# A macaron block on one core: query and key halves laid out through DRAM, with a ring of three loaded batches

## What is computed

```python
x = L0_attn_x                                    # (16, 256, 128)
x = x + 0.5 * ffn_block(layernorm(x))            # phase 0
x = x + linear_attention(layernorm(x))           # phase 1
x = x + 0.5 * ffn_block(layernorm(x))            # phase 2
# ffn_block: h = ln1(x); x += softmax_attention(h), 16 heads of 8, causal;
#            h = ln2(x); x += mixture(h), 8 experts, the best 2 per token, hidden 256
# linear_attention: q, k = elu(.) + 1; sums of k v and of k over the tokens so far,
#            out = (q . sum(k v)) / (q . sum(k)), then Wo
```

## Time and profile before

| | us |
|---|---|
| median of 3 runs | 1413.6 (1412.59 to 1418.59) |
| the profiled execution, its own time | 1418.66 |
| its span, first to last instruction | 1416.9 |
| mean granted TensorE clock, share of full speed | 0.912 |
| busiest engines | DVE 1115.8, PE 1085.8, ACT 839.7, POOL 548.4 |

### The profile page before, as it was taken

How to read it: one execution, slowest core, us unless ns; L and a number is a source line. 1 busy time by engine, 2 the same in 40 slices (tenths; PEclk the granted TensorE clock), 3 DMA queues, 4 the chain that set the end, 5 groups by cost and what they waited for, 6 DMA issues and landing times.

```text
span 1416.9 us, 37025 instructions
## 1 busy us (share of the span) xinstructions
PE 1085.8 (77%) x12412; PEld 819.6 (58%) x12412; DVE 1115.8 (79%) x2411; ACT 839.7 (59%) x1311; POOL 548.4 (39%) x681
## 2 busy tenths in 40 slices
PE   4688888888854998476877868989888888549980
PEld 3566666666643666255655546857666666436660
DVE  6868889999965887677577767779999999658875
ACT  2457777777843555244656544668777787535550
POOL 6620255555563666201000004002555555636661
PEclk9899999999966999688999987999999999769995
DMA  8911111111102332201033310011111111023326
GB/s 292 412 48 38 43 46 49 51 43 51 53 20 61 86 90 69 82 30 34 7 77 79 79 43 19 0 28 45 50 49 45 51 53 47 26 57 88 87 72 187
DMA packets 124880, 98.71 MB, mean 70 GB/s; under 512 B 41584, under 2 KB 116848, under 8 KB 124784
## 3 DMA queue, kind: packets, MB, share of 16 engines
q1 hardware_dynamic: 103216, 72.68, 17.7%
q0 software_dynamic: 9088, 18.76, 4.0%
...
## 4 chain that ended last, share of the span: by engine, by line
DVE 29%; PE 24%; issue 20%; ACT 9%; POOL 6%; DMA 6%; SPq 3%; DVEq 1%; ACTq 1%; POOLq 0%
DVE negm L1058 6%; PE banks L311 4%; POOL ys L1464 4%; SPq L1552 3%; PE banks L293 3%; DVE p_lo L1277 2%; DMA kst<-k_all 2%; DVE negm L1062 2%; ACT pf L866 2%; DVE pf L1284 2%; DVE x_all L1017 2%; PE banks L434 2%; ACT p_hi L732 2%; PE banks L430 2%; PE banks L466 2%
## 5 line engine op out<-in xcount | busy, mean ns | idle before, releaser
L715 ACT ACTIVATE pf<-banks 128x1536 f32<-128x1536 f32 x128 | 185.7, 1451 | 121.0 <-PE banks L455 119.9
L1070 DVE TENSOR_TENSOR p_lo<-pf,p_hi 128x1536 f16<-128x1536 f32 x128 | 223.9, 1749 | 3.2 <-ACT p_hi L732 3.0
L1464 POOL DMA_INDIRECT ys<-q_all,dest x156 | 151.4, 970 | 115.8 <-ACT q_all L872 90.9
L732 ACT CAST p_hi<-pf 128x1536 f16<-128x1536 f32 x128 | 188.7, 1474 | 2.0
L1415 POOL DMA_INDIRECT xs<-n_all,slot x128 | 164.7, 1287 | 54.9 <-issue 37.6
L1058 DVE TENSOR_REDUCE negm<-banks 128x4 f16<-128x1024 f32 x128 | 156.0, 1219 | 28.7 <-PE banks L434 20.3
L1441 POOL TENSOR_SCALAR rs<-mv 128x2 f32<-128x2 f32 x32 | 44.3, 1385 | 346.0 <-DVE mv L1113 295.3
L455 PEld LDWEIGHTS banks<-ident,negm 128*128 128x128 f16 x1536 | 119.7, 99 | 78.1 <-issue 4.4
L455 PE MATMUL banks<-ident,negm 128*128 128x128 f16 x1536 | 150.1, 221 | 0.0
L448 PE MATMUL banks<-qst,kst 128*128 128x512 f16 x384 | 148.1, 386 | 2.1 <-ACT pf L715 2.1
L434 PE MATMUL banks<-kst,qst 128*128 128x128 f16 x1536 | 129.7, 221 | 0.0
...
## 6 DMA issues: line engine op xcount, KB each, us to landing
...
```

The costliest lines, as they stand in the source:

```text
L715: nc.scalar.activation(pf[:, g % 2, :, :, :].rearrange(flat), banks_t[:, :, :].rearrange("p a b -> p (a b)"), ACT.Exp, scale=HD ** -0.5).t ...
L732: nc.scalar.copy(p_hi[:, g % 2, :, :, :].rearrange(flat), pf[:, g % 2, :, :, :].rearrange(flat))\
L1070: nc.vector.tensor_tensor(lo, pf[:, g % 2, :, :, :].rearrange(flat), hi, ALU.subtract)\
L1464: nc.gpsimd.indirect_dma_start(ys, bass.IndirectOffsetOnAxis(ap=dest[:, t % YB, h:h + 1], axis=0), y_out[:, t % YB, h, :], None).then_inc( ...
```

## The change

- `sel`, the spreading matmuls and their four copies are gone; so are `q_all` and `k_all`. A DRAM tensor `qk_d` takes their place, in head order and with three blocks of 8 rows a head instead of four (96 partitions in use of 128, KR).
- In the front, ACT issues 2 stores a batch (one high block of the queries, one of the keys) right after `qk_high`, SP 4 (the other blocks) after `qk_low`: 6 DMAs of 64 KB. The halves have three places (RB).
- The core's tiles have three places, and a load is of a whole batch: 4 + 1 + 1 DMAs, all issued by SP, after `turned` and `values` of the batch three before. SP issues the loads only after the last store of the front. ACT issues none in phase 1's core.
- The front's buffers and banks are doubled; PE turns two batches ahead. DVE's order changes at the start: it waits for the second part of rstd ahead of step 0, computes the third part's statistics in step 1, and waits for it in step 4. In phase 1 `pair_in` stands in even steps. All loops over the front are written out.
- In phase 0 the clears come first on DVE (`qst` with three places, and a tile `zeros` of its own for xs); SP loads w3 and clears xs behind the loads of batches 0 to 2. The wait for the zeros ahead of phase 0 is gone (the scatter's own stays).
- SP issues the last 8 loads of ys of phase 1 between the stores. PE's loop over the core is written over three batches.

```diff
-LOADS = 16 * 5
+RB = 3
+KR = 3 * GH * HD
+STORES = 16 * 6
+LOADS = 16 * 6
...
-        ht = sb("ht", [P, T * P])
-        q_all = sb("q_all", [P, B, G, T * P], F16)
-        k_all = sb("k_all", [P, B, G, T * P], F16)
+        xn = sb("xn", [P, 2, T, P])
+        ht = sb("ht", [P, 2, T * P])
         v_all = sb("v_all", [P, B, T, H, VC], F16)
-        kst = sb("kst", [P, G, T * P], F16)
-        qst = sb("qst", [P, G, GH, T * P], F16)
-        v_hl = sb("v_hl", [P, T, H, VC], F16)
+        kst = sb("kst", [P, RB, G, T * P], F16)
+        qst = sb("qst", [P, RB, G, GH, T * P], F16)
+        v_hl = sb("v_hl", [P, RB, T, H, VC], F16)
+        zeros = sb("zeros", [P, ZR * RW])
+        x_nats = sb("x_nats", [P, XB, 2, RW])
...
-        qk_hi, qk_lo = [a[:, :, :, :, :].rearrange("p a b c d -> p (a b c d)")[:, 0:2 * 2 * T * P]
-                        .rearrange("p (n k m) -> p n k m", n=2, k=2) for a in (p_hi, p_lo)]
+        qk_hi, qk_lo = [a[:, :, :, :, :].rearrange("p a b c d -> p (a b c d)")[:, 0:RB * 2 * T * P]
+                        .rearrange("p (n k m) -> p n k m", n=RB, k=2) for a in (p_hi, p_lo)]
...
+        qk_d = nc.dram_tensor("qk_d", [B, 2, G * GH, 3, HD, T * P], F16).ap()
...
             def front_qk(ph, b):
-                if not (isinstance(b, int) and b == 0):
-                    pe.wait_ge(ph["qk_out" if ph["soft"] else "full_in"], b)
+                if b >= 2:
+                    pe.wait_ge(ph["qk_out" if ph["soft"] else "full_in"], b - 1)
                 for k in range(2):
-                    ins = nc.tensor.matmul(psum[2][:, k * 256:(k + 1) * 256], w_qk[ph["w"]][:, k, :], ht[:, :],
-                                           start=(k == 0), stop=True, skip_group_check=True)
+                    ins = nc.tensor.matmul(psum[2 + 3 * (b % 2)][:, k * 256:(k + 1) * 256], w_qk[ph["w"]][:, k, :],
+                                           ht[:, b % 2, :], start=(k == 0), stop=True, skip_group_check=True)
                 ins.then_inc(ph["qk_done"], 1)
-            def front_spread(ph, b, buf):
-                pe.wait_ge(ph["qk_out"], b + 1)
-                for k in range(2):
-                    for g in range(G):
-                        n = 2 * k + g // 2
-                        if g % 2 == 0 and n in (0, 3) and not (isinstance(b, int) and b == 0):
-                            if n == 0:
-                                pe.wait_ge(ph["act_spread"], ph["n"] * (3 * B) + b * 3)
-                            else:
-                                pe.wait_ge(ph["dve_spread"], ph["n"] * B + b)
-                        bank = (psum[3:] + [bank_pv])[n]
-                        for part, src in enumerate((qk_hi, qk_lo)):
-                            ins = nc.tensor.matmul(bank[:, g % 2 * 256:(g % 2 + 1) * 256],
-                                                   sel[:, k, part, g, :, :, :].rearrange("p a b c -> p (a b c)"),
-                                                   src[:, buf, k, :], start=(g % 2 == 0 and part == 0),
-                                                   stop=(part == 1), skip_group_check=True)
-                        if g % 2:
-                            ins.then_inc(ph["spread_done"], 1)
...
+            def front_step(ph, b):
                 front_v(ph, b)
                 front_qk(ph, b)
-                if not (ph["soft"] or first or second):
-                    front_carry(ph, b - 2, buf)
-                if not last:
-                    front_turn(ph, b + 1)
-                if not first:
-                    if not ph["soft"]:
-                        front_keys(ph, b - 1, 1 - buf)
-                    front_spread(ph, b - 1, 1 - buf)
-                    if not ph["soft"]:
-                        front_state(ph, b - 1, 1 - buf)
+                if not ph["soft"] and b >= 2:
+                    front_carry(ph, b - 2, b % 2)
+                if b + 2 < B:
+                    front_turn(ph, b + 2)
+                if not ph["soft"] and b >= 1:
+                    front_keys(ph, b - 1, (b - 1) % 2)
+                    front_state(ph, b - 1, (b - 1) % 2)
             def front(ph):
...
+            def batch_in(ph, place):
+                ring, n = place
+                pe.wait_ge(ph["loaded"][ring], LOADS * (used(ph, ring, n) + 1))
+            def natural(ph, b, g, place):
                 mask = maskb[:, :, :].rearrange("p a b -> p (a b)")
                 later = not (isinstance(b, int) and b == 0 and g == 0)
-                pe.wait_ge(ph["qk_loaded"][g // 2], ph["n"] * (LOADS * B) + LOADS * (b + 1))
+                if g == 0:
+                    batch_in(ph, place)
...
+                for b in range(4):
+                    iteration(ph, b, at_batch(b), place=b)
+                with pe.Fori(0, (B - 7) // RB) as i:
+                    for n in range(RB):
+                        iteration(ph, i * RB + (4 + n), at_loop(i, n))
+                for b in range(B - 3, B):
+                    iteration(ph, b, at_batch(b), last=(b == B - 1))
+                at = at_batch(B - 1)
...
-            def spread_out(ph, b, which=range(3)):
-                for n in which:
-                    dst, part = (q_all, k_all)[n // 2], n % 2
-                    sc.wait_ge(ph["spread_done"], ph["n"] * (4 * B) + 4 * b + n + 1)
-                    nc.scalar.copy(dst[:, b, 2 * part:2 * part + 2, :].rearrange("p a b -> p (a b)"),
-                                   psum[3 + n][:, :]).then_inc(ph["act_spread"], 1)
...
+                if b >= RB:
+                    sc.wait_ge(ph["stored"][ring], STORES * used(ph, ring, b // RB))
...
+            def store_high(ph, b):
+                sc.wait_ge(ph["hi_in"], ph["n"] * B + b + 1)
+                for k in range(2):
+                    nc.scalar.dma_start(qk_d[b, k, :, 0, :, :], qk_hi[:, b % RB, k, :])\
+                        .then_inc(ph["stored"][b % RB], 16)
...
+            def front_step(ph, b):
+                v_high(ph, b)
...
+                qk_high(ph, b)
+                store_high(ph, b)
...
+                for ring in range(RB):
+                    sc.wait_ge(ph["stored"][ring], STORES * used(ph, ring, len(range(ring, B, RB))))
...
-            def next_k(ph, b, hf):
-                gs = slice(2 * hf, 2 * hf + 2)
-                nc.scalar.dma_start(kst[:, gs, :], k_all[:, b + 1, gs, :]).then_inc(ph["qk_loaded"][hf], 16)
...
+            def front_step(ph, b):
                 if not ph["soft"] and b >= 2:
                     state_own(ph, b - 2)
                 v_low(ph, b)
-                if not last:
-                    front_ht(ph, b + 1)
-                if not (last or before_last):
-                    front_norm(ph, b + 2)
-                qk_elu(ph, b, buf)
-                qk_low(ph, b, buf)
-                if not first:
-                    spread_out(ph, b - 1)
+                if b + 2 < B:
+                    front_ht(ph, b + 2)
+                if b + 3 < B:
+                    front_norm(ph, b + 3)
+                qk_elu(ph, b)
+                qk_low(ph, b)
...
             def front(ph):
                 if ph is phases[0]:
+                    flat = "p n a b c -> p (n a b c)"
+                    nc.vector.memset(qst[:, :, :, :, :].rearrange(flat).bitcast(F32), 0.0)
+                    nc.vector.memset(v_all[:, :, :, :, HD:HD + 1].rearrange("p a b c d -> p (a b c) d"), 1.0)
+                    nc.vector.memset(zeros[:, :], 0.0).then_inc(cleared, 1)
                     ve.wait_ge(x_in[0], 16)
                 front_stats(ph, 0)
-                if ph is phases[0]:
-                    nc.vector.memset(v_all[:, :, :, :, HD:HD + 1].rearrange("p a b c d -> p (a b c) d"), 1.0)
-                    nc.vector.memset(qst[:, :, :, :].rearrange("p a b c -> p (a b c)"), 0.0).then_inc(cleared, 1)
                 ve.wait_ge(ph["rstd"], 1)
                 front_norm(ph, 0)
+                front_norm(ph, 1)
                 if ph is phases[0]:
                     ve.wait_ge(w_in, weights_in)
                 front_ht(ph, 0)
-                front_norm(ph, 1)
+                front_norm(ph, 2)
+                front_ht(ph, 1)
                 if ph is phases[0]:
                     ve.wait_ge(x_in[1], 16)
                 front_stats(ph, 1)
-                front_step(ph, 0, 0, first=True)
-                front_stats(ph, 2)
                 ve.wait_ge(ph["rstd"], 2)
-                for start, end in ((1, 5), (5, B - 3)):
-                    if start > 1:
+                for b in range(B):
+                    if b == 1:
+                        front_stats(ph, 2)
+                    if b == 4:
                         ve.wait_ge(ph["rstd"], 3)
-                    with ve.Fori(start, end, 2) as b:
-                        front_step(ph, b, 1)
-                        front_step(ph, b + 1, 0)
-                front_step(ph, B - 3, 1)
-                front_step(ph, B - 2, 0, before_last=True)
-                front_step(ph, B - 1, 1, last=True)
-                spread_out(ph, B - 1)
```

(62 more changed lines are left out.)

283 lines of the change are left out of this document (89 added, 194 removed).

## The result

The changed kernel takes 1429.98 us (median of 4 runs, 1428.95 to 1432.02), the kernel before 1413.1 beside it: ratio 1.0112, 95% interval 1.0085 to 1.014. It is **slower by 1.1%**, where 1385 and faster was forecast. The profiled execution has a span of 1430.3 us.

What follows compares the result with a forecast made beforehand. No engine bounds the whole, so stages were summed: phase 0 +3, phase 1's front −12 and core −14, phase 2's front −1 and core −5: −29 from 1418.7, 1389.7 profiled, 1385 us as median; range 1361 to 1412.

Steps and rivals of the forecast that it cites:

- Phase 1's core: Phase 1's core: waits for query loads and ACT's load issues go, a batch takes 7.9 us in place of 8.8: −14.
- rival A: Phase 1's core: PE, DVE and ACT wait for each other whatever the loads do; gives 2, not 14: 1397; chance 0.16.
- its end of −22: Phase 1's core: the best end of the range around −14, at DVE's bound (6.9 us a batch with its gaps).
- phase 1's core still at 138: Phase 1's core: one of the signs listed beforehand that would show the forecast wrong.
- Rival B: Soft fronts: PE, now with gaps, stays at 1.2 GHz and nothing is gained there: +18, 1403; chance 0.12.
- The stores' issue: Soft fronts: SP takes 0.55 us to issue a store, so a step takes 2.35 us in place of 3.28.
- Rival C: Fronts: stores take 1.0 us to issue and SP's stores become the bound: +43, 1428; chance 0.10.
- Phase 0: Phase 0: front 6 earlier, then PE stands still 16 us for load 3 behind the clears: +3 (ends −6 and +14).
- PE waiting for `loaded` once: Phase 0's core, batch 3: a listed sign of being right, 10 to 20 us and nowhere else.
- the 9.4: Phase 0's core: POOL's split of w3, 9.4 us, might block DVE's L1070; covered by waiting for load 3, nothing added.
- Phase 1's front: Phase 1's front: a pair of steps takes 12.6 us in place of 15.7: −12 (ends −18 and −3).
- Phase 2: Phase 2: front −1 (ends −7 and +8); core −5 (ends −9 and 0), as SP's loads are two batches ahead.

Runs made afterwards that it cites:

- e12_before_later: The kernel before, with the context turned behind the fourth scores in phase 1's core, in PE's and ACT's order: 1397.85 us, ratio 0.9887.
- e15: The changed kernel with 1 added matmul that nobody reads ahead of each wait for `cx` in phase 1's core: 1425.28 us, ratio 1.0096.
- e16: The changed kernel with 3 added matmuls that nobody reads ahead of each wait for `cx` in phase 1's core: 1414.04 us, ratio 1.0002.
- e6: The changed kernel with 5 added matmuls that nobody reads ahead of each wait for `cx` in phase 1's core: 1414.92 us, ratio 1.0015.
- e1: The changed kernel, with phase 1's score matmuls contracting all 128 partitions (the last 32 zeros) in place of 96: 1430.54 us, ratio 1.0092.
- e14: The changed kernel, with ACT again issuing 4 DMAs a batch in phase 1's core, to a DRAM tensor nobody reads: 1429.45 us, ratio 1.0099.

## Why the prediction was wrong

- **Phase 1's core: the step that failed, in cause and in sign.** "PE waited 11.7 us for query loads … Both go … I take 7.9: −14." The waits did go, and a batch at the full clock stayed at 8.2 to 8.3 us. A wait that ends last is no proof that it holds the work: e12_before_later makes the loads' waits vanish without touching a load. This is rival A, which I gave 0.16; its argument, "The loads were late only because the batch was", was right. The sum itself took 141 us by 16, start and end included, and so read 8.8 a batch off a period that was 8.2 to 8.3; and its end of −22 doesn't follow from 6.9 a batch, which gives 141 − 110 = 31. On top, the clock fell in 10 batches of 14, no longer in 3. The fourteen periods grew by 9.5 us together (121.4 to 130.9); the other 2.2 of the +11.7 lie in start and end (the stretch to the first `cx` took 13.0 us at a granted clock of 0.81, before 11.7 at 1.00). The prediction's own sign of being wrong, "phase 1's core still at 138", came, at 154. Rival B had the clock, but placed it in the soft fronts, where I had looked at its effect on steps; I did not ask of the core what PE's clock does once its idle time lies in one piece. Shown: work put ahead of that stretch brings the clock back (e15, e16, e6), and neither the rows (e1) nor ACT's issues (e14) do. That the kernel before kept its clock because query loads held PE up on the way to the wait for `cx` fits the table, but not batch by batch (its clock fell at waits of 0.91 and 0.86 us and behind a query wait of 1.65, and not at 1.34), and no run puts such waits back alone: it stays argued.
- **The stores' issue.** Taken at 0.55, between 0.5 and 0.75; it was 0.62, spaced 0.64, so SP needs 2.6 us a batch, not 2.35. In phase 2 the last steps came 2.4 us apart on average (forecast 2.35), since the ring of three hid SP's delay at first. But SP fell behind: the last store was issued by 929.7, 4.9 behind the last `qk_low`, not 2.3. From the last `qk_low` to the core: 11.6, 8.4 and 10.4 us in the three phases, where I had 8.3 for all. The term is mis-sized by 2 to 3 us in the soft phases, although load 0 was issued faster than I had it (2.7 us in phase 2, not 3.9; landing took 2.6, not 2.1). Rival C named the mechanism, at 1.0 us per issue.
- **Phase 0.** Core +10.8 against +9: right in its mechanism, and partly by luck in its size, since a shorter stall met a later start. The stall in batch 3 was 10.8 us, not 16, and "PE waiting for `loaded` once, in batch 3 of phase 0, for 10 to 20 us" is the row at 161.71. That POOL's split of w3 blocks DVE's L1070 (now L1023) was left open and is shown now:

```profile
109.87 3.91 DVE L1023 TENSOR_TENSOR p_lo<-pf,p_hi 128x1536 f16<-128x1536 f32 x1 [0.59 <-ACT p_hi L712]
...
115.44 4.23 DVE L1023 TENSOR_TENSOR p_lo<-pf,p_hi 128x1536 f16<-128x1536 f32 x1
...
121.32 1.74 DVE L1023 TENSOR_TENSOR p_lo<-pf,p_hi 128x1536 f16<-128x1536 f32 x1
```

  Two took 4.7 us longer in all, while POOL's split ran from 108.54 to 118.05: half of the 9.4 that the prediction had priced. They end at 119.7, long before PE stands still for load 3 (150.9 to 161.7), so the stall covers them. The front gave 0.6 of its 6: the last `qk_low` came at 87.3, not 85, the core at 98.8, not 93.
- **Phase 1's front.** −4.4 against −12. A pair of steps took 14.0 us (five, 610.25 to 680.07), not 12.6: 8.5 to 8.7 for the step behind `pair_in`, which keeps PE and so ACT's exp waiting for 3.8 us, and 5.1 to 5.8 for the other. Five pairs make 7 us of the miss; the last four steps took 5.0 each (forecast 4.8). The experts ahead of it are as before: 151.5 and 151.8 us from the core's end to the first `pair_in`.
- **Phase 2.** Front +0.1 against −1 and core −4.4 against −5: right as sums. The front's is two misses that nearly cancel: the last `qk_low` came 61.7 us after the front's start (forecast 62.5), the core 10.4 behind it (forecast 8.3).

The Trainium skill, page "SBUF — State Buffer", section "Who interferes with whom", says that a DVE instruction with two SBUF inputs contends with a GpSimd one that reads SBUF; the three rows above agree (3.91 and 4.23 against 1.74 us). Its page "TensorE: Matmul & The Clock Gate", section "A second HAM failure mode: psum-queue depth-cycling", tells of a kernel whose PE is idle for short times between groups and whose clock goes to and fro. Phase 1's core agrees in this: PE stands still for 1.4 us a batch, its clock goes to and fro, and the filler runs give the price here, 16 us in 154.
